# A linear-attention block that masks its queries once for each tile on GpSimd and takes its scores from 32 rows

## What is computed

```python
q = l2norm(silu(short_conv(hidden @ Wq.T, conv_q)))      # likewise k; v without the norm
def step(W, chunk):                                      # chunks of 16 tokens, W is 8 x 8 per head
    inter = einsum('bqhk,bhkv->bqhv', q_c, W)
    qk = einsum('bqhd,bkhd->bhqk', q_c, k_c) * mask      # causal
    intra = einsum('bhqk,bkhv->bqhv', qk, v_c)
    W_new = W + einsum('bchk,bchv->bhkv', k_c, v_c)
    return W_new, inter + intra
```

## Time and profile before

| what | value |
|---|---|
| median of 3 runs | 3739.61 us (3732.49 to 3739.84) |
| profiled execution, its own time | 3741.74 us |
| its span in the trace | 3740.4 us |
| PE busy | 3130.3 us (84%) |
| DVE busy | 2584.6 us (69%) |
| ACT busy | 2196.5 us (59%) |
| POOL busy | 1512.7 us (40%), 1308 instructions |

### The profile page before, as it was taken

How to read it: one execution, slowest core, us unless ns; L and a number is a source line. 1 busy time by engine, 2 the same in 40 slices (tenths; PEclk the granted TensorE clock), 3 DMA queues, 4 the chain that set the end, 5 groups by cost and what they waited for, 6 DMA issues and landing times.

```text
span 3740.4 us, 53498 instructions
## 1 busy us (share of the span) xinstructions
PE 3130.3 (84%) x18885; PEld 1842.4 (49%) x19000; DVE 2584.6 (69%) x6180; ACT 2196.5 (59%) x4819; POOL 1512.7 (40%) x1308
## 2 busy tenths in 40 slices
PE   3677697989889999889899877879888888889866
PEld 1244284747544555445555433547465756534422
DVE  3879977474888777667777889976654455556522
ACT  2444445243565777567677664856486756767633
POOL 2545555443455553214655665663303321112100
PEclk9789999999999999999999988999999999999855
DMA  5122142223100010220100011344423543232110
GB/s 210 44 78 65 45 128 76 77 59 90 56 23 1 1 31 8 73 50 14 49 1 10 15 37 36 106 115 122 110 67 106 157 134 92 62 83 51 36 25 5
DMA packets 193604, 238.34 MB, mean 64 GB/s; under 512 B 36984, under 2 KB 154168, under 8 KB 191288
## 3 DMA queue, kind: packets, MB, share of 16 engines
q1 hardware_dynamic: 169016, 157.43, 14.9%
q0 software_dynamic: 24320, 77.47, 6.8%
HBM read 183.61 MB, written 53.74 MB: 63 GB/s over the span
## 4 chain that ended last, share of the span: by engine, by line
PE 35%; DVE 15%; ACT 11%; POOL 5%; issue 4%; SPq 2%; DMA 1%; DVEq 0%; POOLq 0%; ACTq 0%
PE psum L326 31%; ACT scratch L370 7%; DVE scratch L392 6%; PE psum L342 4%; POOL scratch L460 3%; ACT L362 3%; DVE scratch L414 3%; DVE scratch L405 2%; SPq L480 2%; DVE scratch L410 1%; DVE scratch L397 1%; DVE scratch L401 1%; POOL scratch L466 1%; DVE scratch L418 1%; ACT w_early L370 1%
## 5 line engine op out<-in xcount | busy, mean ns | idle before, releaser
L370 ACT ACTIVATE scratch<-psum 128x512 f32<-128x512 f32 (+7 forms) x1812 | 842.7, 494 | 804.2 <-PE psum L326 643.5
L326 PE MATMUL psum<-scratch 128*128 128x128 f32 (+16 forms) x8016 | 935.2, 323 | 123.2 <-ACT scratch L370 40.2
L460 POOL TENSOR_TENSOR scratch<-scratch 128x512 f32<-128x512 f32 (+3 forms) x536 | 706.3, 1331 | 668.5 <-PE psum L326 228.1
L370 ACT ACTIVATE scratch<-scratch 128x255 f32<-128x255 f32 (+11 forms) x1368 | 623.5, 480 | 552.6 <-DVE scratch L405 246.7
L326 PEld LDWEIGHTS psum<-scratch 128*32 128x32 f32 (+9 forms) x8016 | 592.6, 147 | 478.6 <-issue 212.0
L326 PE MATMUL psum<-scratch,w_constants 128*128 128x512 f32 (+2 forms) x848 | 454.7, 630 | 25.7 <-ACT scratch L370 18.8
L362 ACT ACT_TABLE_LOAD x333 | 427.2, 1283 | 31.8 <-PE psum L326 15.0
L405 DVE TENSOR_TENSOR_SCAN scratch<-scratch 128x512 f32<-128x512 f32 x256 | 420.5, 1644 | 16.6 <-POOL scratch L460 13.9
L392 DVE TENSOR_TENSOR scratch<-scratch,psum 128x512 f32<-128x512 f32 (+2 forms) x532 | 309.0, 586 | 138.6 <-PE psum L326 94.7
L342 PE MATMUL psum<-w_constants,scratch 128*128 128x128 f32 (+3 forms) x1880 | 326.2, 294 | 85.8 <-POOL scratch L460 37.2
L326 PE MATMUL psum<-scratch,w_early 128*128 128x512 f32 (+12 forms) x912 | 297.7, 466 | 74.4 <-DVE scratch L392 47.8
(11 more groups left out here) (106 smaller groups left out, 4219.9 us busy)
## 6 DMA issues: line engine op xcount, KB each, us to landing
scratch<-b_out SPq DMA_DIRECT2D x80, 384.0 KB
slots_out<-scratch SPq DMA_DIRECT2D x112, 128.0 KB, 2.4
q_stack<-scratch SPq DMA_DIRECT2D x72, 192.0 KB, 2.8
scratch<-q_out SPq DMA_DIRECT2D x96, 96.0 KB
scratch<-slots_in SPq DMA_DIRECT2D x16, 512.0 KB
q_out<-scratch SPq DMA_DIRECT2D x40, 192.0 KB, 2.9
scratch<-slots_in SPq DMA_DIRECT2D x16, 448.0 KB
scratch<-q_stack SPq DMA_DIRECT2D x24, 288.0 KB
```

The source lines that it names most:

```text
L326: return self.engine.matmul(out, lhsT, rhs, start=start, stop=stop, **kw)
L370: return self.engine.activation(out, src, function, **kw)
L460: return self.engine.tensor_tensor(out, a, b, op)
```

## The change

The mask no longer tells which of 16 heads a row belongs to but which of the four heads of its group (`head_of_row`, 128 x 4). One `qm` for a tile then serves all four groups, because group g's rows are 32g to 32g+31: PE takes `k` and `qm` on these 32 rows alone. `qm` is now doubled over tiles.

```diff
-    c["channels_of_head"] = (np.arange(HEADS8)[None] == ch[:, None] // HD8).astype(float)
+    c["head_of_row"] = (np.arange(4)[None] == ch[:, None] % 32 // HD8).astype(float)
...
             for g in range(4):
                 rows = slice(32 * g, 32 * g + 32)
-                e.wait_ge(*(yield self["one_head", t, g]))
+                if g == 0:
+                    e.wait_ge(*(yield self["one_head", t]))
...
-                e.matmul(self.a, self.k[:, here], self.qm[g % 2].rearrange("p a b -> p (a b)")).then_inc(*self.post("scores", t, g))
+                e.matmul(self.a, self.k[rows, here], self.qm[t % 2][rows].rearrange("p a b -> p (a b)")).then_inc(*self.post("scores", t, g))
...
     def pool(self, e):
         e.wait_ge(*(yield self["normed", "k"]))
-        for n in range(4 * TILES):
-            t, g = divmod(n, 4)
-            if n >= 2:
-                e.wait_ge(*(yield self[("scores", *divmod(n - 2, 4))]))
+        for t in range(TILES):
+            if t >= 2:
+                e.wait_ge(*(yield self["scores", t - 2, 3]))
             q = self.q[:, t * P:(t + 1) * P]
-            e.tensor_tensor(self.qm[g % 2], over(q.unsqueeze(1), [P, 4, P]),
-                            over(self.c["channels_of_head"][:, 4 * g:4 * g + 4].unsqueeze(2), [P, 4, P]), ALU.mult).then_inc(*self.post("one_head", t, g))
-            if g == 0:
-                e.wait_ge(*(yield self["token", "v_tok"]))
-                if t:
-                    e.wait_ge(*(yield self["intra", t - 1, 3]))
-                e.tensor_tensor(self.vm, over(self.v_tok[:, t:t + 1, :], [P, 4, P]), v2(self.c["head_of_col_group"], P), ALU.mult).then_inc(*self.post("spread_v", t))
+            e.tensor_tensor(self.qm[t % 2], over(q.unsqueeze(1), [P, 4, P]),
+                            over(self.c["head_of_row"].unsqueeze(2), [P, 4, P]), ALU.mult).then_inc(*self.post("one_head", t))
+            e.wait_ge(*(yield self["token", "v_tok"]))
+            if t:
+                e.wait_ge(*(yield self["intra", t - 1, 3]))
+            e.tensor_tensor(self.vm, over(self.v_tok[:, t:t + 1, :], [P, 4, P]), v2(self.c["head_of_col_group"], P), ALU.mult).then_inc(*self.post("spread_v", t))
```

## The result

The change makes the kernel slower: 3830.2 us at the median (3824.1 to 3838.0) against 3739.7, a ratio of 1.0243, 95% interval 1.0219 to 1.0267. The forecast was 3723, and the measured time lies 70 us above the top of the range.

A forecast was written before the change was run, and what follows sets the result against it. The prediction took PE, busy 84% of the span, to be the limit rather than POOL. Its terms, -6 + 4 - 15 = -17 us, gave 3723 us against a median of 3739.6; the range was 3702 to 3760.

The forecast's parts named there:

- What bounds the kernel: Whole span: PE busy 84%, POOL only 5% of the chain that ended last; 50 us less POOL need not save 50.
- 48 multiplies fewer: Linear blocks, POOL: -6 us, all from the first linear stretch (415 to 545 us); ends 0 and -40.
- The long DVE operation of the earlier trace: Near 450 us: a 128x32 DVE multiply took 4.15 us beside three POOL multiplies; none should take 4 us afterwards.
- My other sign: First linear stretch: DVE's 128x512 scan, 1672 ns on the mean, gets shorter; if not, the direct term is 0.
- Scores from 32 rows: The 64 score matmuls on PE, 70.7 us in all: a 32-row matmul takes as long, so 0 saved.
- Waits: PE loses three of four waits for POOL's masked copies, worth at most 0.7 us; taken as zero.
- Table loads: ACT: 12 more loads of 1283 ns, 15.4 us, 26% on the chain: +4 us, ends 0 and +15.4.
- R3: Rival: added table loads on ACT's in-order queue are on the path, no gain at the end: 3749 us; chance 0.18.
- Fewer `bf_masks` matmuls: PE: 26 fewer, 8.4 us, where PE was planned idle; taken as 0, with -8.4 as one end.
- R4: Rival: PE's clock in the linear stretch falls from 0.99 to 0.91, +26 us, 3764 us; chance 0.11.
- The new order: End of the kernel: last stream alone about 115 us, not 147; -15 us, ends 0 and -32.
- R1: Rival: POOL holds up DVE in both linear stretches, -40 us direct, giving 3700 to 3705 us; chance 0.10.

The follow-up runs named there:

- e6: Kernel before's order, one masked copy (qm) a tile but scores over all 128 rows, against the kernel before: ratio 0.9985.
- e5: Kernel before's order, four masked copies a tile kept, scores from 32 rows, against the kernel before: ratio 1.0025.
- e1: The whole change with every engine's queue in the kernel before's order, against the kernel before: 3750.9 us, ratio 1.0012.
- e15: Changed kernel, same order to about 958 us, then the planner counts DVE 2000 ns later once: 3757 us, ratio 1.0032.
- e2: Changed kernel in its own order, but scores over all 128 rows: ratio 1.0198 to the kernel before.
- e7: Changed kernel in its own order with 1015 filling bf_masks matmuls in place of 622: ratio 1.0223 to the kernel before.
- e11: Kernel before with the planner's DMA-queue account 20 ns later, giving another order of the same work: ratio 0.9890.
- e14: Changed kernel, same order to about 958 us, then the planner counts DVE 1000 ns later once: 3855 us, ratio 1.0301.
- e4: Changed kernel with the planner's DMA-queue account 47 ns later, giving another order of the same work: ratio 1.0008 to the kernel before.
- e13: Changed kernel, same order to about 958 us, then the planner counts DVE 500 ns later once: 3802 us, ratio 1.0166.
- e16: Changed kernel, same order to about 958 us, then the planner counts DVE 3000 ns later once: 3832 us, ratio 1.0245.
- e9: Changed kernel with the planner's DMA-queue account 20 ns later, giving another order of the same work: ratio 1.0034 to the kernel before.
- e10: Changed kernel with the planner's DMA-queue account 100 ns later, giving another order of the same work: ratio 1.0107 to the kernel before.
- e8: Kernel before in its own order with every third filling bf_masks matmul left out, 432 in place of 648: ratio 1.0068.

## Why the prediction was wrong

**What bounds the kernel.** Right that POOL does not: the linear blocks do not gain from its 48 multiplies.

**48 multiplies fewer, -6.** The size agrees: 0.9985 in the old order is 6 us. Its place does not: the first linear stretch was to give it, and in e6 the addition to x at 579.3 us is 0.1 us late, that of 931 us 0.5 us early, and the end 2.5 us late. So as far as the trace shows, the agreement is luck. POOL's group is at 32 and 1092 ns, as said. The long DVE operation of the earlier trace rows took 4.15 us beside three of the block's multiplies (4.18 in e5, which has all four masks), 3.16 in the changed kernel beside two, and 2.18 in e1 and e6 beside one; that event was as read, about 1 us for each multiply. My other sign was poor: the scan's mean of 1672 ns is 1604 after, 1659 in e6 and 1582 in e5. It does not follow the number of masks.

**Scores from 32 rows, 0.** Too low, by 9 us in the old order; the 17 in the new one are not clear of noise. The matmul is about as priced, 647 ns in e1 and e5 against 637 before (666 in the changed kernel, at its lower clock). What was not priced is the neighbour, the next 128-row weight load and its matmul, which start 0.09 to 0.39 us later for each score. The Trainium skill (TensorE: Matmul & The Clock Gate, Why this matters for your kernels) says that one matmul of K=32 takes the time of one of K=128; the trace agrees within 10 ns for the matmul by itself, 647 and 637 ns, and not for the pair of it and what follows.

**Waits, 0.** As said: from 624 to 985 us others waited 0.6 us for these multiplies in e1, and 1.9 us in the changed kernel.

**Table loads, +4.** Their count does not tell a good order: 324 to 393 of them show no relation to the time. e15 has 60 more than the kernel before, 77 us were all on the path, and is 12 us slower. R3 named the right side, slower, with a mechanism that could give 15 us of the 90 at most.

**Fewer `bf_masks` matmuls, and R4.** The clock of the linear stretch did fall, to 0.96, below the 0.97 that I had named, but not for R4's reason: with 32-row scores in the old order it stays at 0.99 (e1, e5), and with 128-row scores in the new one it is 0.95 (e2). And e7 shows that giving it back returns little; R4 took its cost from PE's whole busy time, as if every matmul were on the path.

**The new order, -15: the step that failed.** The tail went as read: 113 us alone by the prediction's measure, to the end of the span, where it said 115. Even the -15 is about what the tail gave back, from 111 us of lateness at 3200 us to 96 at the end. What failed is the zero beside it: the prediction took "for granted that nothing earlier is late in turn, which the order can't tell", and the order made the changed kernel 111 us late by 3200 us. In place of a gain of 15 us the order cost 1.98% (e2) to 2.3% (the changed kernel against e1), 74 to 87 us. The runs also show how wide the term's bounds should have been. I gave it 0 to -32; orders of the same work lie from -44 us (e11 against the kernel before) to +104 (e14 against e1). The lateness was named at the end as the thing not costed, and then kept out of the range.

**R1** fell: the linear blocks end later, and in e6 0.5 us sooner. The rule of the Trainium skill behind it stands in another section of the page than the prediction names (SBUF — State Buffer, SBUF: two separate sides): a VectorE instruction with two SBUF inputs and a GpSimd instruction that reads SBUF shut each other out, and whichever starts first keeps the port for its whole instruction. The event fits it as far as the multiply of VectorE waits for whole GpSimd instructions: it took 4.15, 3.16 and 2.18 us, and began while GpSimd's scan product was running. But it did not get its turn after that one instruction; it waited for the block's three, two and one multiplies behind it as well. What the rule is worth here is the 0 to 11 us of e6.

**What stays open.** Which waits make the difference between a good order and a poor one. In the changed kernel from 620 to 1000 us POOL waits longer for others, a view of its waits:

```profile
POOL scratch L466 <- DMA slots_out<-scratch: 53.1, 3, 35.0
POOL slots_in L466 <- DVE scratch L392: 41.6, 2, 41.5
```

In e4, which is the same work and 26 us less late there, the first is 39.4 us, 19.6 at the longest, and the second is missing from the list. That is a place to look, not a cause shown. Nor is it shown whether the order up to 958 us makes the ones behind it worse: the four that share it (e13 to e16) took 3812 us in the mean, three free orders of the same work (e4, e9, e10) 3759, and both sets scatter by more than 25 us.

## What to carry to other kernels

Where a planner fixes the order of several mixed streams, try each version in several orders of its own, or hold the order and test the work, before a change is judged: here the work costs 0.1%, within the noise, and the order 2.3%, which 47 ns in one account give back. Small shifts of such a number are also a cheap search: one of three other orders of the old work was 1.1% faster than the kernel before. That a matmul on fewer rows takes no longer by itself does not make it free; look at the weight load that comes after it.

## What the runs showed that I had not expected

A 32-row fp32 matmul of 512 columns takes 647 ns, a 128-row one 637 ns, but the matmul behind a 32-row score starts 518 ns after the score's second record and not 432. Where scores and 128-row matmuls alternate, the period goes from 1.08 to 1.47 us. And a mean clock of 0.909 in place of 0.929, 152 us more at 1.2 GHz, cost 25 us where the order stayed (e8), in a program with PE busy for 84% of the span.
